# Graph attention on one core: gathered rows added by the DMA engines in SBUF, and the sums' one-hot matrix made by a comparison on VectorE

## What is computed

```python
k = layer_norm(x_node @ Wk); v = layer_norm(x_node @ Wv); q = layer_norm(x_node @ Wq)      # per head
ke = layer_norm(x_edge @ Wke); ve = layer_norm(x_edge @ Wve)
rel_k = layer_norm(concat([ke, k[src]]) @ relk_W + relk_b)
qk = sum(q[dst] * rel_k, -1) / 4
lse = log(segment_sum(exp(qk), dst))                       # with the maximum taken out
rel_v = layer_norm(concat([ve, v[src]]) @ relv_W + relv_b)
agg = segment_sum((qk - lse[dst]) * rel_v, dst)
z = layer_norm(relu(agg @ z_W + z_b));  out = layer_norm(x + z)
```

## Time and profile before

| | |
|---|---|
| median of 3 runs | 3204.89 us (3204.49 to 3209.08) |
| the profiled execution | 3209.04 us |
| its span, first to last instruction | 3207.3 us |
| TensorE (matmul) busy | 2937.6 us, 92% |
| VectorE busy | 2978.3 us, 93% |
| ACT busy | 2307.1 us, 72% |
| GpSimd busy | 2576.2 us, 80% |
| granted TensorE clock | 0.975 |

### The profile page before, as it was taken

The page is one execution under the profiler, slowest core; times in us unless marked ns, Lnnn a source line. Parts: engine busy times, 40 slices in busy tenths (PEclk is TensorE's granted clock), DMA queues, the critical chain, the costliest instruction groups (busy, mean ns, idle before and its releaser), DMA issues. The chain is left out here.

```text
span 3207.3 us, 75878 instructions
## 1 busy us (share of the span) xinstructions
PE 2937.6 (92%) x18674; PEld 2485.6 (77%) x18870; DVE 2978.3 (93%) x3387; ACT 2307.1 (72%) x5276; POOL 2576.2 (80%) x2622
## 2 busy tenths in 40 slices
PE   5669999999999999999999999999999999996955
PEld 3358888888888888888888888888888888885633
DVE  7879999999999999999999999999999999996957
ACT  2457777777777777777777777777777777775536
POOL 7768888888888888888888888888888888883773
PEclk9989999999999999999999999999999999999976
DMA  3568887778787778777778777778777777785642
GB/s 86 160 180 237 240 243 240 242 238 243 239 243 239 243 238 243 239 243 240 241 239 244 238 244 238 243 238 244 239 242 240 241 240 241 242 246 176 178 123 76
DMA packets 660921, 715.95 MB, mean 223 GB/s; under 512 B 97993, under 2 KB 554430, under 8 KB 660469
## 3 DMA queue, kind: packets, MB, share of 16 engines
q1 hardware_dynamic: 568201, 499.33, 51.8%
q0 software_dynamic: 84896, 211.42, 21.8%
q10 hardware_dynamic: 7756, 4.43, 0.6%
HBM read 482.62 MB, written 231.46 MB: 223 GB/s over the span
## 5 line engine op out<-in xcount | busy, mean ns | idle before, releaser
L1301 POOL DMA_INDIRECT e_rows<-node_table,e_gcol x1564 | 2093.0, 1338 | 422.2 <-issue 419.9
L1123 PE MATMUL banks<-w_edge,e_eat 128*128 128x240 f32 x6256 | 1435.9, 373 | 57.9 <-DVE e_p L1408 50.6
L1123 PEld LDWEIGHTS banks<-w_edge,e_eat 128*128 128x128 f32 x6256 | 1156.7, 190 | 281.2 <-DVE e_p L1408 207.1
L1116 PE MATMUL banks<-e_h,e_oh 128*128 128x248 f32 x3128 | 805.5, 380 | 9.4 <-ACT e_agg L1200 5.3
L1399 DVE TENSOR_REDUCE e_zs<-e_z 128x96 f32<-128x1440 f32 x391 | 646.1, 1653 | 40.2 <-DVE e_z L1389 7.8
L1209 ACT ACTIVATE e_oht<-banks 128x512 bf16<-128x512 f32 x391 | 233.5, 597 | 476.8 <-remote 240.2
L1116 PEld LDWEIGHTS banks<-e_h,e_oh 128*128 128x128 f32 x3128 | 533.6, 190 | 43.5 <-DVE e_h L1416 6.2
L1200 ACT ACTIVATE e_agg<-banks 128x496 f32<-128x496 f32 x782 | 455.3, 582 | 95.7 <-PE banks L1116 95.7
L1408 DVE TENSOR_TENSOR e_p<-banks,e_yr 128x960 f32<-128x960 f32 x391 | 448.8, 1148 | 3.3 <-PE banks L1123 3.3
L1416 DVE TENSOR_TENSOR e_h<-e_p,e_zw 128x960 f32<-128x960 f32 x391 | 448.9, 1148 | 1.2 <-POOL e_zw L1314 1.2
L1371 DVE TENSOR_TENSOR e_p<-e_p,e_rows 128x960 f32<-128x960 f32 x391 | 449.1, 1149 | 0.0
(11 more groups left out here) (413 smaller groups left out, 2596.6 us busy)
## 6 DMA issues: line engine op xcount, KB each, us to landing
tile_sums<-e_agg SPq DMA_DIRECT2D x391, 496.0 KB
e_q<-q_by_rank SPq DMA_DIRECT2D x1564, 96.0 KB
e_ea<-in_edge_attr SPq DMA_DIRECT2D x390, 256.0 KB
e_rows<-node_table,e_gcol POOLq DMA_INDIRECT x1564
edge_lse<-t_lse_sb SPq DMA_DIRECT2D x14, 448.0 KB, 3.6
edge_qk<-e_qkt SPq DMA_DIRECT2D x130, 48.0 KB
node_table<-n_tb SPq DMA_DIRECT2D x24, 240.0 KB, 2.8
n_x<-in_x SPq DMA_DIRECT2D x24, 128.0 KB, 2.3
```

Source lines behind the costliest of these rows:

```text
L1116: last = nc.tensor.matmul(agg_ps[:, (j % 2) * AW:(j % 2 + 1) * AW], oh[:, x % OR, j, :], hh[:, x % HR, j, :, :].rearrange("p h e -> p (h e ...
L1123: last = nc.tensor.matmul(out_ps[:, j // 2, (j % 2) * 2 * HC:(j % 2 + 1) * 2 * HC], eat[:, x % 4, j * P:(j + 1) * P], t["w_edge"][:, at:at ...
L1301: g.indirect_dma_start(out=rows[:, k, j, :], out_offset=None, in_=table, in_offset=bass.IndirectOffsetOnAxis(ap=gcol[:, kb, at:at + 1].bit ...
```

## The change

The gathers no longer write to `e_rows`, which is gone, but add to `p` itself in SBUF (`compute_op=ALU.add`). For that a row of the table gets p's form, 256 numbers (1024 bytes) with a zero in each 16th place; the gathers go to lag 4, all four together, behind a wait for p (`s_p`), and their readers wait for `s_ga`. VectorE's addition L1371 is gone. ACT's squares go to lag 6, L1389 and L1399 to lag 7, L1265, L1274 and L1275 to lag 8; L1321 goes from GpSimd at lag 8 to VectorE at lag 9, L1314 from GpSimd to VectorE at lag 9. `e_oh` is made on VectorE at lag 6 by comparing `place` (0 to 127 along the row) with the edge's rank in its tile; TensorE's L1172 and ACT's L1244 are gone. e_oht's steps go to lag 5, q's expansion to lag 6, q's loads to lag 2. `cols` carries the ranks beside the sources, which costs 13 transposes and four copies before the loop; index loads are twice as long for each partition. The order on VectorE becomes: dot product's first part (qk0), product with q, qk, sums (zs), second weight (w2), p, hh, yvar, comparison.

```diff
-        table = dram("node_table", [N, 2 * HC])
+        table = dram("node_table", [N, 2 * F])
-        cols = sb_mid("cols", [P, ROWS], i32)
+        cols = sb_mid("cols", [P, 2, ROWS], i32)
...
+            dve.wait_ge(s_srct, 1)
+            link(v.memset(tb[:, :, :, :, C:D], 0.0))
...
+                    dve.wait_ge(s_rkc, 4)
+                    v.memset(t["cols"][PART_E:P, 1, FULL_T:FULL_T + 1].bitcast(f32), OUT_RANK)
+                    v.memset(t["cols"][:, 1, FULL_T + 1:BATCHES * BATCH * TILES].bitcast(f32), OUT_RANK)
...
+            act.wait_ge(s_rkt, 1)
+            for i in range(4):
+                n = min(4, KT - 4 * i)
+                sc_.activation(rank_by_part[:, 4 * i:4 * i + n, :], src_ps[i].rearrange("e (k p) -> e k p", p=P), ACT.Copy).then_inc(s_rkc, 1)
...
             pick(1)
+            pe.wait_ge(s_srcc, 4)
+            pe.wait_ge(s_rank, 1)
+            for k in range(KT):
+                last = nc.tensor.transpose(src_ps[k // 4][:, (k % 4) * P:(k % 4 + 1) * P], rank[:, k, :], ident[:])
+            last.then_inc(s_rkt, 1)
...
# edges, SP
-                            sp.wait_ge(s_ohp, used)
-                            sp.wait_ge(s_pt, used)
+                            sp.wait_ge(s_ohtp, used)
+                            sp.wait_ge(s_oh, used)
+                            sp.wait_ge(s_psq, used)
...
-                x = c - 1
+                x = c - 2
...
# edges, TensorE
-                x = c - 4
+                x = c - 5
...
-                    if loop or x >= 2:
-                        pe.wait_ge(s_oh, n - 1)
-                    elif x == 1:
-                        pe.wait_ge(s_oht, 1)
+                    if loop or x >= 1:
+                        pe.wait_ge(s_oht, n)
...
-                    for j in range(TILES):
-                        at = (x % BATCH) * GE + j * P
-                        last = nc.tensor.matmul(misc[:, j * P:(j + 1) * P], feat[:, kb, at:at + P], t["nfeat"][:], start=True, stop=True)
-                    last.then_inc(s_ohp, 1)
...
# edges, ACT
-                x = c - 5
+                x = c - 6
...
-                    act.wait_ge(s_pt, n + 1)
+                    act.wait_ge(s_ga[k], 64 * use(x, i, PR))
...
-                    act.wait_ge(s_ohp, n + 1)
-                    if loop or x >= OR:
-                        act.wait_ge(s_agg, 2 * (n - OR) + 2)
-                    nc.scalar.activation(oh[:, x % OR, :, :].rearrange("p j n -> p (j n)"), misc, ACT.Relu).then_inc(s_oh, 1)
...
# edges, GpSimd
-                        if loop or x >= RR:
-                            pool.wait_ge(s_pt, n - RR + 1)
+                        pool.wait_ge(s_p, n + 1)
...
-                        g.indirect_dma_start(out=rows[:, k, j, :], out_offset=None, in_=table,
-                                             in_offset=bass.IndirectOffsetOnAxis(ap=gcol[:, kb, at:at + 1].bitcast(u32), axis=0),
-                                             bounds_check=last_node, oob_is_err=True).then_inc(s_ga[k], 16)
+                        g.indirect_dma_start(out=p[:, k, j, :, :, :].rearrange("p h k d -> p (h k d)"), out_offset=None, in_=table,
+                                             in_offset=bass.IndirectOffsetOnAxis(ap=gcol[:, kb, 0, at:at + 1].bitcast(u32), axis=0),
+                                             bounds_check=last_node, oob_is_err=True, compute_op=ALU.add).then_inc(s_ga[k], 16)
...
-                gathers(c - 3, i, loop, 0)
...
-                gathers(c - 3, i, loop, 2)
-            every(pool, body, GROUPS + 9)
+                gathers(c - 4, i, loop, 0)
+                gathers(c - 4, i, loop, 2)
+            every(pool, body, GROUPS + 4)
...
# edges, VectorE
-                    v.tensor_tensor(out=p[:, k, :, :, :, 0:C].rearrange("p t h k c -> p (t h k) c"), in0=p[:, k, :, :, :, 0:C].rearrange("p t h k c -> p (t h k) c"),
-                                    in1=rows[:, x % RR, :, :].rearrange("p t (h c) -> p (t h) c", c=C), op=ALU.add).then_inc(s_pt, 1)
...
+                x = c - 9
+                    dve.wait_ge(s_zr, n + 1)
+                    v.tensor_tensor(out=qk0[:], in0=zs[:, x % WR, :, 2 * H:3 * H], in1=zr[:, x % WR, :, 0:H], op=ALU.mult).then_inc(s_qk0, 1)
...
+                x = c - 9
+                    dve.wait_ge(s_qk, n + 1)
+                    dve.wait_ge(s_zw, n + 1)
+                    v.tensor_tensor(out=zw[:, x % WR, :, :, 1], in0=hh[:, x % HR, :, :, 2 * C], in1=zw[:, x % WR, :, :, 0], op=ALU.mult).then_inc(s_w2, 1)
...
+                x = c - 6
+                    v.tensor_tensor(out=oh[:, x % OR, :, :], in0=place[:].unsqueeze(1).to_broadcast([P, TILES, P]),
+                                    in1=gcol[:, kb, 1, at:at + TILES].bitcast(f32).unsqueeze(2).to_broadcast([P, TILES, P]), op=ALU.is_equal).then_inc(s_oh, 1)
```

More of the change, by code:

```diff
@@ L390, in _ @@
                     sp.wait_ge(s_tb, n + 1)
-                    sp.dma_start(table[P * b:P * b + nb * rows, :].rearrange("(b p) f -> p b f", p=rows), tb[0:rows, n % 3, 0:nb, :]).then_inc(s_tst[n % 3], 16)
+                    sp.dma_start(table[P * b:P * b + nb * rows, :].rearrange("(b p) f -> p b f", p=rows),
+                                 tb[0:rows, n % 3, 0:nb, :, :].rearrange("p b h d -> p b (h d)")).then_inc(s_tst[n % 3], 16)
             for k in range(3):
@@ L709, in _ @@
                     dve.wait_ge(s_u, n + 1)
-                    v.tensor_tensor(out=tb[0:rows, n % 3, 0:nb, :], in0=tb[0:rows, n % 3, 0:nb, :],
-                                    in1=t["table_bias"][0:rows].unsqueeze(1).to_broadcast([rows, nb, 2 * HC]), op=ALU.add).then_inc(s_tb, 1)
+                    v.tensor_tensor(out=tb[0:rows, n % 3, 0:nb, :, 0:C], in0=tb[0:rows, n % 3, 0:nb, :, 0:C],
+                                    in1=t["table_bias"][0:rows].rearrange("p (h c) -> p h c", c=C).unsqueeze(1).to_broadcast([rows, nb, 2 * H, C]), op=ALU.add).then_inc(s_tb, 1)
                 n = c - 2
@@ L718, in _ @@
                         dve.wait_ge(s_tst[n % 3], 16 * (n // 3))
-                    v.tensor_tensor(out=tb[0:rows, n % 3, 0:nb, :].rearrange("p b (h c) -> p b h c", c=C),
+                    v.tensor_tensor(out=tb[0:rows, n % 3, 0:nb, :, 0:C],
                                     in0=second[n % 2][0:rows, 0:nb * 2 * HC].rearrange("p (b h c) -> p b h c", b=nb, c=C),
@@ L953, in edges @@
     feat = t["feat"]
-    gcol = sb("e_gcol", [P, FB, BATCH * TILES], i32)
+    gcol = sb("e_gcol", [P, FB, 2, BATCH * TILES], i32)
+    place = sb("e_place", [P, P])
     ysq = sb("e_ysq", [P, 2, TILES, 2 * HC])
@@ L958, in edges @@
     yr = sb("e_yr", [P, 2, TILES, 2 * H])
-    rows = sb("e_rows", [P, RR, TILES, 2 * HC])
     p = sb("e_p", [P, PR, TILES, H, 2, D])
@@ L979, in edges @@
     b_i = spare[:, at_i + 320:at_i + 320 + CB * H].bitcast(i32).rearrange("p (b h) -> p b h", h=H)
+    place_i = spare[:, at_i + 400:at_i + 400 + P].bitcast(i32)
     firsts, ends, oc, same_c, same_b, cen = t["firsts"], t["ends"], t["oc"], t["same_c"], t["same_b"], t["cen"]
@@ L988, in edges @@
     s_q = [sem(f"q_loaded{i}") for i in range(QR)]
-    s_ga = [sem(f"gathered{i}") for i in range(RR)]
+    s_ga = [sem(f"rows_added{i}") for i in range(PR)]
     s_sst = [sem(f"sums_stored{i}") for i in range(AG)]
@@ L1336, in link @@
                 dve.wait_ge(s_ch, done[0])
-            dve.wait_ge(s_k, 5)
+            dve.wait_ge(s_k, 6)
+            link(v.tensor_copy(out=place[:], in_=place_i))
             link(v.tensor_tensor(out=ends[:, 1:2], in0=t["ends_f"][:, 1:2], in1=t["ends_f"][:, 0:1], op=ALU.not_equal))
@@ L1365, in body @@
             def body(c, i, loop):
-                x = c - 5
+                x = c - 9
+                if is_group(x, loop):
+                    n = UNROLL * i + x
+                    dve.wait_ge(s_zr, n + 1)
+                    if loop or x >= 1:
+                        dve.wait_ge(s_qk, n)
+                    v.tensor_tensor(out=qk0[:], in0=zs[:, x % WR, :, 2 * H:3 * H], in1=zr[:, x % WR, :, 0:H], op=ALU.mult).then_inc(s_qk0, 1)
+                x = c - 7
                 if is_group(x, loop):
                     n, k = UNROLL * i + x, x % PR
-                    dve.wait_ge(s_ga[x % RR], 64 * use(x, i, RR))
-                    dve.wait_ge(s_p, n + 1)
-                    v.tensor_tensor(out=p[:, k, :, :, :, 0:C].rearrange("p t h k c -> p (t h k) c"), in0=p[:, k, :, :, :, 0:C].rearrange("p t h k c -> p (t h k) c"),
-                                    in1=rows[:, x % RR, :, :].rearrange("p t (h c) -> p (t h) c", c=C), op=ALU.add).then_inc(s_pt, 1)
+                    dve.wait_ge(s_ga[k], 64 * use(x, i, PR))
+                    dve.wait_ge(s_qx, n + 1)
+                    if loop or x >= ZR:
+                        dve.wait_ge(s_z, n - ZR + 1)
+                        dve.wait_ge(s_qk, n - ZR + 1)
+                    v.tensor_tensor(out=z[:, x % ZR, :, 2 * H:3 * H, :], in0=p[:, k, :, :, 0, :],
```

(13 more changed lines are left out.)

56 lines of the change are left out of this document (25 added, 31 removed).

## The result

The changed kernel takes 3541.8 us (median of 4 runs, 3532.14 to 3552.4) beside 3205.47 for the kernel before: a ratio of 1.105 (95% interval 1.101 to 1.108), slower by a tenth where 5% faster was forecast. The profiled execution took 3552.4 us, its span is 3550.6 (before 3209.04 and 3207.3).

A forecast was written before the change was run, and what follows sets the result against it. VectorE was taken to bound the loop at 6.95 us a turn; its new sum of 6.36, taken as 6.5, gave 391 x (6.95 - 6.5) = 176, less 2: 3035 or 3031 us, likeliest 2976 to 3093, 8-in-10 range up to 3490.

The forecast's parts named there:

- the unknown: Loop's adding gathers: GpSimd 1.03 us each to at most double, DMA 1.67 to 3.33 us a turn; taken near lower end.
- VectorE's 6.36 us: VectorE's summed turn in the loop after removing the addition and gaps, adding comparison and products: 6.36 us, from 6.95.
- the 0.13 taken: Price of each small VectorE instruction in the new order, with something standing between it and its user: 0.13 us.
- TensorE's "6.57 at most": TensorE's need in a loop turn once four matmuls go: 6.79 - 0.22 = 6.57 us at most, perhaps 6.46.
- The taken 6.5 us: Forecast loop turn: VectorE's sum with a little for the meeting with TensorE, 6.5 us.
- take 2: Added transposes, copies, memsets and wider table before the loop: transposes and copies hidden, 0 to 6 us in all, 2 taken.
- GpSimd's stretching: Loop gathers lengthened beside VectorE's two-operand instructions: up to 0.95 us for one, some 0.35 for another, 1.30 a turn.
- The landing that was to have 3.2 us to spare: Last gather of a group lands 8.0 us after p, ACT squares it 11.2 us after p: 3.2 us spare.
- Rival 2: GpSimd writing gather descriptors becomes bound: 1.52 us a gather, 7.28 to 7.7 us a turn, 3334 to 3490 us; chance 0.28.
- at half as much again: Adding gather's descriptor writing on GpSimd costs half more: 1.52 us a gather, 7.28 us a turn before stretching.
- double the price: Adding gather's descriptor writing on GpSimd doubles: 9.28 us a turn, 4116 us; left out of the 8-in-10 range.
- Rival 1: The 16 DMA engines become the loop's bound: 7.26 us a turn, +121 us, 3326 us; chance 0.21.

## Why the prediction was wrong

**The step that failed** is "the unknown", where the prediction says of an accumulating gather that "No row shows one". The trace of the kernel before has no such gather, but thirteen indirect DMAs that add, in the stage after the loop: line L1552 adds the carried sums into tile_sums by the same kind of instruction (`indirect_dma_start` with `compute_op=ALU.add`, 128 rows) the other way round, from SBUF into HBM. And L478, ahead of the loop, is one that writes rows to HBM without adding.

```profile
L1552 POOL DMA_INDIRECT tile_sums<-firsts,carry_idx x13: 1556/1663/2020, 2970.5 to 2994.8; - x13
L478 POOL DMA_INDIRECT q_by_rank<-room_b,rank_row x49: 972/977/2562, 119.8 to 190.9; - x49
```

The shortest adding one is 1556 ns, 0.58 us over the plain one beside it; the changed loop's is 1550, 0.54 over its plain form. With L1552's price the sum would have been 4 x (1.56 + 0.30) = 7.44 us on GpSimd, 0.49 over the turn of before, at least 190 us slower. I bounded the price from the gathers of the loop, 1.03 to twice that, and took the lower end because a plain gather is "the nearest row"; the nearest was the one with the same operation, and it lay outside the stage that I read.

**The other terms, one by one.**
- VectorE's 6.36 us: 6.36 in the changed kernel's turn without a stop, 6.35 on average in the plain gathers of 64 rows. The comparison takes 0.68 us (L1433), as L626 in the earlier trace rows. The small products cost 0.10 and 0.12 us for the 0.13 taken, and L1382 0.17 for its 0.13, so the sum came out in part by small errors that cancel.
- TensorE's "6.57 at most", perhaps 6.46: it is less, since with plain gathers of 64 rows the loop turns in 6.35 with the same matmuls.
- The taken 6.5 us: 6.69 with whole plain gathers. The median turn is 6.35; what lies over it are the long turns above, which the prediction didn't have and which are unexplained.
- Ahead of the loop: "take 2", and it was 1.4 us less. All hidden, as said. Behind the loop 17.8 us were missing in the sum: some 5 for a group that gathers after its p (292.7 for 288.1 with plain gathers), the rest for GpSimd being late.
- GpSimd's stretching: 1.30 us a turn predicted, 0.87 + 0.40 in the turn shown of the plain gathers of 64 rows, 0.73 on their average. The landing that was to have 3.2 us to spare had them: with whole plain gathers ACT waited for a gather once, for 1.0 us. In the changed kernel ACT waits 357 times, because GpSimd is behind by more than any spare time.
- The Trainium skill (SBUF — State Buffer, "Who interferes with whom") infers that tensor_tensor leaves descriptor writing alone. The rows of the runs say otherwise again: 1.83 us for 0.96 beside L1416.

**The rivals.** Rival 2 is what happened, and its condition, "at half as much again", was near the size: 1.55 us against 1.52. Its top of 7.7 us a turn was 0.08 too low (stretching, 7.78 - 7.43 = 0.35) and the tail of 17.8 us wasn't in it, so that 3541.8 lies 52 us above the range. (Its turn at double the price should read 4 x (2.06 + 0.30) = 9.44 us, not 9.28; the range left that case out either way.) Its argument "part of the 1.02 us may be fixed" was right in a way that didn't help: the fixed part is the larger, and by the lines through 64 and 128 rows it is the part that the addition raises most.

Rival 1 came true as a load but not as the bound. It put the gathers' queue at 3.33 us of a turn at most; it is 3.72. That and the loads make 7.66 us, and yet lightening the engines to 84% brought only 0.26 us, and to 80% with half rows 0.06. The Trainium skill's rule (Collectives: The Full Stack, "The bandwidth ceiling: the fold count and why AG ≠ RS ≠ AR"), by which two source reads halve the rate, agrees in its factor: 1520 us of the 16 engines' time against 790 for the same rows without adding, 1.9 times. By the rule this rival "is the outcome"; the runs say that GpSimd is. Had GpSimd been faster, the engines could have been the next bound, at up to 7.7 us a turn (worked out from the shares, in which slowing by contention may be counted; not run). If so, either alone would make the change slower, and I had given each a chance of its own, as if only one could be there.

## What to carry to other kernels

Price an operation by a row that has the same operation before one that has the same shape, and look for it in the whole trace, not only in the stage that changes. Moving work from a busy engine into a DMA moves it to the engine that writes the descriptors, too: if that one issues without a pause (here 5.33 of 6.95 us before any stretching), an increase of a few tenths of a us an instruction decides the matter. And try the free part of a change by itself: two instructions moved so that none waits for its neighbour brought 2%, while the change, whose new order does the same among much else, lost 10%.

## What the runs showed of the hardware that I had not expected

- An adding gather costs GpSimd 1.55 us for 128 rows of 1 KB and 1.55 for rows of 512 bytes; by a line through 64 and 128 rows, 1.28 us fixed and 2.1 ns a row, against 0.90 and 0.8 ns for a plain one.
- It is stretched where it starts inside L1416, with two operands in SBUF (2.12 us on average, up to 2.56), and nowhere else in the changed kernel between 600 and 2600 us (1.55 to 1.61), though the DMA engines are busy for 0.98 of the time throughout.
- It moves each row as one packet, where a plain gather packs four: 235040 packets against 84896 in the queue for the same 224.23 MB, and 1.9 times the time of the DMA engines.
- A loop can fetch code in every pass (five packets of 8 KB). Of two kernels that do, one has long turns that cost 0.3 us a turn, the other none; that the fetches cause them isn't shown. What brings the fetches is open; it isn't the number of VectorE's instructions.
